# A preceding attention layer with a mixture of experts: the router on an exact fp32 input, the shared expert last, and all engines' orders rewritten

## The chip, the cores and the metric

The kernel runs on one core of a Trainium2 chip. Its time is the device time of one execution in microseconds; 136.29 us is the median of three runs of the kernel before (136.12 to 136.59).

## The reference

x has shape (2, 1024, 128), fp32. Two pre-normed blocks follow each other.

```python
x = x + attention(layernorm(x))   # 4 heads, q/k 32 wide with rotary, v 64 wide
# retention: o = (q k^T * decay_mask) v, rms-normalised per head, gated by silu(x Wg^T), times Wo^T
x = x + ffn(layernorm(x))
def ffn(x):
    shared = silu(x @ sh_up_w + sh_up_b) @ sh_down_w + sh_down_b
    scores = softmax(x @ gate_w.T)                # 8 experts
    topk_w, topk_i = top_k(scores, 2); topk_w = topk_w / topk_w.sum()
    comb = one_hot(topk_i) weighted by topk_w     # (tokens, 8)
    y = sum over e of comb[:, e] * (silu(x @ up_w[e] + up_b[e]) @ down_w[e] + down_b[e])
    return y + shared
```

## The kernel before, in words

The 1024 positions of the two sequences are cut into four groups (g = 0 to 3) of four tiles of 128 tokens; a pair (g, p), p = 0 or 1, is the same 128 positions of both sequences. Every engine has its own program: a list of calls of small functions, written out by hand in one order for each engine (POOL from L394, ACT from L550, DVE from L934, PE from L1290). Semaphores join them. In PE's list an `after(signal, g, p)` waits for a signal before the call behind it; most such waits are there so that a PSUM bank is free again. The dictionary `PLACE` (L48) says in which PSUM bank the result of each attention step goes, `OWN` (L63) where it goes otherwise.

Attention, for each pair: `x1_t` transposes the normed input on PE, ACT's `x1_hi` copies it from PSUM rounded to fp32r (XH1), DVE's `x1_lo` writes the rest (XL1). `proj_qk`, `proj_v` and `proj_g` each make three fp32r matmuls per tile (high by high, high by low, low by high: `product`, L1100 to L1104). Rotary and `rotate` are on DVE, `qk_t` transposes (PE) and ACT's `qk_sb` copies. Then `scores` (PE, bank set bA), `masked` (DVE, reads bA), `attend` (PE, writes bA), `squares` (ACT) and `gate_out` (DVE), which both read bA; the next `scores` waits for `gate_out` (`after(ogr, ...)`). POOL does the reciprocal roots and `normalize_out`, then come `out_t` (PE), `transposed_out` (ACT), `proj_out` (PE), `add_attention` (DVE).

Experts, for each group: `stats2`, the norm, `x2_t` on PE, `x2_hi` on ACT (L498, fp32r copy XH2) and `x2_lo` on DVE (L821, XL2). `router` (L1208) multiplies each of the four tiles, as the stationary operand, with the router weights: two fp32r matmuls per tile, XH2 by the 16 columns GWS (high and low) and XL2 by the 8 high ones. `route_a` (L826) adds the two parts of the logits on DVE and takes the maximum off, `exps` on ACT makes the exponentials, `rank` and `route_b` on DVE choose two experts and make the weights CMB and CX, `comb_t` (PE) transposes them, `comb_rows` and `comb_sb` (ACT) copy them out. SP broadcasts the rows through DRAM into CB (`widen`, L295). `up_proj(g, k)`, k = 0 to 8, makes three fp32r matmuls with 512 columns, ACT's `hidden` applies SiLU, DVE's `gating` multiplies by CB. k = 0 is the shared expert, which takes no weight (`expert`, L242). `down_proj` adds all nine in bank bY by fp32 matmuls. ACT's `sums`, PE's `y_t` and DVE's `result` give the output of groups 0 to 2.

Group 3 has another ending. `down_last` (L1236) multiplies tile by tile, tokens on the partitions. The shared expert (k = 0) and the biases (`bias`, L1259) go to bY; `base` (L898) adds the residual X into YS; `mix(3, k)`, k = 1 to 8 (L904), adds each routed expert's product from bank k mod 4 of bA, scaled by its column of CMB, four DVE instructions (L922) per expert, the last ones into OUT. `store_last(0)` and `store_last(1)` (L313) send the halves from the SP queue.

In ACT's list `exps` needs the exponential table and the `hidden` behind it the SiLU table: each change is an ACT_TABLE_LOAD.

Of the kernel before, what the change touches and what calls it, by code (L numbers as in the profile page):

```python
# [40 lines left out]
TABLES = 6  # L41
# [56 lines left out]
def retention_moe_kernel(nc, x, wqkvg, wot, gnw, upw, upb, dnw, dnb, gatew, const, rotary_tables, scratch, out):  # L98
    ctx = ExitStack()
    with ctx:  # L100
# [6 lines left out]
        def sig(name, per=1):  # L107
# [18 lines left out]
        GWS = sb("GWS", [P, 2, E], F32R)  # L126
# [36 lines left out]
        XL2 = sb("XL2", [P, 2, GC], F32R)  # L163

# [19 lines left out]
        YS = sb("YS", [P, GC])  # L184
        OUT = sb("OUT", [P, 2, TILES, P])
# [14 lines left out]
        w_ex_hi, gw_lo, uw_lo, wog, db_hi, db_lo = (  # L200
            sig(n) for n in ("w_ex_hi", "gw_lo", "uw_lo", "wog", "db_hi", "db_lo"))
# [15 lines left out]
        biased, based, mixed, last_half, tail = (sig(n) for n in ("biased", "based", "mixed", "last_half", "tail"))  # L217
# [24 lines left out]
        def expert(k):  # L242
            return E if k == 0 else k - 1
# [20 lines left out]
        def _(sp):  # L264
# [61 lines left out]
            store_last(1)  # L326
# [4 lines left out]
        def _(pool):  # L331
# [73 lines left out]
            rstd1(3, 1)  # L405
            rms(0, 1)
            normalize_out(0, 1)
            rms(1, 0)
            normalize_out(1, 0)
            rstd2(0, 0)  # L410
            rstd2(0, 1)
            rms(1, 1)
            normalize_out(1, 1)
            rstd2(1, 0)
# [5 lines left out]
            rstd2(2, 0)  # L420
            rms(3, 0)
            rstd2(2, 1)
            normalize_out(3, 0)
            rms(3, 1)
            normalize_out(3, 1)
            rstd2(3, 0)
# [3 lines left out]
        def _(act):  # L430
# [67 lines left out]
            def x2_hi(g, p):  # L498
                act.wait_ge(t4.sem, t4.at(g, p))
                act.copy(XH2[:, g % 2, two(p)], place("x2_t", g, p)[:, 0:2 * P]).then_inc(xh2.sem, 1)  # L500

            def hidden(g, k):
                e = expert(k)
# [34 lines left out]
            def split_experts():  # L538
                act.wait_ge(ld_gw.sem, 16)
                act.copy(GWS[:, 0, :], GW[:, :])  # L540
                act.wait_ge(ld_up.sem, 16)
                act.copy(UWH[:, :], UW[:, :]).then_inc(w_ex_hi.sem, 1)

            def split_biases():
# [3 lines left out]
                act.wait_ge(ld_ub.sem, 16)  # L548

# [14 lines left out]
            gates(1, 0)  # L564
            split_biases()
            x1_hi(1, 1)
            squares(0, 0)
            values(1, 0)
            values(1, 1)
            qk_sb(1, 0)  # L570
            x1_norm(2, 0)
            x1_norm(2, 1)
            gates(1, 1)
            x1_hi(2, 0)
            transposed_out(0, 0)
# [74 lines left out]
            hidden(2, 5)  # L650
            x2_norm(3, 0)
            hidden(2, 6)
            x2_norm(3, 1)
            x2_hi(3, 0)
            x2_hi(3, 1)
            hidden(2, 7)
            hidden(2, 8)
# [5 lines left out]
            hidden(3, 3)  # L663
            hidden(3, 4)
            comb_sb(3)
# [3 lines left out]
            hidden(3, 8)  # L669

        @block.vector
        def _(dve):
# [153 lines left out]
            def route_a(g):  # L826
                parts = bM[:, 0:TILES * 2 * E].rearrange("r (m s e) -> r m s e", s=2, e=E)
                dve.wait_ge(logits.sem, logits.at(g))
                dve.tensor_reduce(LG[:, :, :], parts.rearrange("r m s e -> r m e s"), AX.X, ALU.add).then_inc(route_a_step.sem, 1)
# [68 lines left out]
            def base(g):  # L898

                dve.wait_ge(biased.sem, 1)  # L900
                dve.wait_ge(yt.sem, yt.at(g - 1))
                dve.tensor_tensor(YS[:, :], bY[:, :], X[:, g * GC:(g + 1) * GC], ALU.add).then_inc(based.sem, 1)

            def mix(g, k):  # L904
                if k == 1:
                    dve.wait_ge(based.sem, 1)
                    dve.wait_ge(route_b_step.sem, route_b_step.at(g, 4))
                if k < E:
                    dve.wait_ge(down.sem, down.at(g, k))
# [181 lines left out]
        def _(pe):  # L1091
# [116 lines left out]
            def router(g):  # L1208
                pe.wait_ge(xl2.sem, xl2.at(g, 1))
                if g == 0:  # L1210
                    pe.wait_ge(gw_lo.sem, 1)
# [378 lines left out]
```

## Time and profile before

| | us |
|---|---|
| median of three runs | 136.29 |
| the profiled execution | 136.48 |
| its span in the profile | 134.7 |
| PE busy | 128.8 |
| DVE busy | 102.9 |
| ACT busy | 81.2 |
| POOL busy | 43.6 |

The span runs from the first to the last thing that the profile shows; 1.8 us of the execution lie outside. PE is the matmul engine, PEld its weight loads, DVE the vector engine, ACT the scalar engine, SP the engine that issues most DMAs. A busy PE record contains the matmul's pipeline, so records overlap: what one matmul costs in a stream is the distance from its start to the next start. One fp32 matmul stands as two records with a weight load each (`proj_out` makes 4 matmuls for each of 8 pairs, and L1197 has 40 + 16 + 8 = 64 records), one fp32r matmul and one transpose as one. The chain of waits gives, from the last instruction backwards, which piece of work set the time.

### The profile page before, as it was taken

The numbers are of one execution on the slowest core, as the hardware profiler recorded it, in microseconds if no ns is written. First come the engines' busy times: TensorE is split into PE (matmuls) and PEld (weight loads), VectorE is DVE, ScalarE is ACT, GpSimd is POOL, SyncE is SP. The second block draws the span as 40 slices with busy tenths as digits, with TensorE's granted clock in tenths as the row PEclk, the third lists the DMA queues.
The fourth block names the chain that finished last, engine by engine and source line by source line (L and its number), as shares of the span: only waits on it lengthen the run. The fifth ranks groups of instructions, "written<-read, shape, count | busy, mean of one in ns | idle before, by whom it ended". The sixth has DMA issues, their size and how long they took to land.

```text
span 134.7 us, 3595 instructions
## 1 busy us (share of the span) xinstructions
PE 128.8 (96%) x1359; PEld 101.7 (76%) x1359; DVE 102.9 (76%) x318; ACT 81.2 (60%) x146; POOL 43.6 (32%) x64
## 2 busy tenths in 40 slices
PE   5999899999999999999999999999999999999990
PEld 5897798999899988978665588566676557489980
DVE  3889999999999999995997728966249437425983
ACT  3359959677506369977848355977454834980230
POOL 6534599390707738264321107000004200000000
PEclk9999999999999999999999999999999999999998
DMA  4999900000000000009900593000961100002002
GB/s 108 290 372 336 335 24 0 5 0 7 5 0 5 0 5 0 2 12 287 339 1 5 146 403 136 21 0 27 324 277 40 42 2 0 0 15 65 5 0 78
DMA packets 8661, 12.53 MB, mean 93 GB/s; under 512 B 1298, under 2 KB 5676, under 8 KB 8644
## 3 DMA queue, kind: packets, MB, share of 16 engines
q1 hardware_dynamic: 8212, 11.84, 26.4%
q10 hardware_dynamic: 432, 0.46, 1.2%
q8 instruction: 11, 0.18, 0.5%
q14 instruction: 6, 0.05, 0.1%
HBM read 11.20 MB, written 1.10 MB: 91 GB/s over the span
## 4 chain that ended last, share of the span: by engine, by line
PE 81%; DVE 7%; ACT 4%; DMA 4%; issue 2%; ACTq 1%; DVEq 0%
PE bY L1281 16%; PE bU L1102 9%; PE bU L1104 8%; PE bU L1103 8%; PE bA L1178 6%; PE bA L1254 5%; DMA W<-wqkvg 4%; PE bU L1197 3%; PE bA L1146 2%; PE bA L1172 2%; PE bU L1138 2%; PE bY L1102 1%; PE bM L1215 1%; PE bM L1197 1%; PE bM L1217 1%
## 5 line engine op out<-in xcount | busy, mean ns | idle before, releaser
L509 ACT ACTIVATE HB<-bU,UB 128x512 f32<-128x512 f32 x36 | 24.6, 687 | 22.2 <-PE bU L1104 21.5
L884 DVE TENSOR_TENSOR HG<-CB,HB 128x512 f32<-128x512 f32 x24 | 16.9, 719 | 11.1 <-ACT HB L509 7.2
L1281 PE MATMUL bY<-HG,DW 128*128 128x512 f32 x48 | 24.6, 594 | 0.0
L1102 PE MATMUL bU<-XH,UWH 128*128 128x512 f32 x36 | 22.6, 628 | 0.2 <-ACT HB L509 0.2
L355 POOL TENSOR_TENSOR RR<-SS,NHALF 128x8 f32<-128x8 f32 x8 | 13.1, 1642 | 17.3 <-DVE SS L779 17.2
L1103 PE MATMUL bU<-XL,UWH 128*128 128x512 f32 x36 | 14.2, 395 | 0.0
L1104 PE MATMUL bU<-XH,UWL 128*128 128x512 f32 x36 | 14.2, 394 | 0.0
L369 POOL TENSOR_SCALAR VE<-MV 128x2 f32<-128x2 f32 x8 | 2.2, 281 | 29.2 <-DVE MV L804 29.2
L1102 PEld LDWEIGHTS bU<-XH,UWH 128*128 128x128 f32 x36 | 6.8, 189 | 5.4 <-issue 4.9
L760 DVE TENSOR_TENSOR SC<-bA,MASK 128x512 f32<-128x512 f32 x16 | 10.2, 680 | 0.1
L484 ACT ACTIVATE SQ<-bA 128x512 f32<-128x512 f32 x8 | 4.8, 598 | 8.9 <-PE bA L1178 8.9
L1103 PEld LDWEIGHTS bU<-XL,UWH 128*128 128x128 f32 x36 | 6.8, 190 | 4.1 <-issue 4.1
L1281 PEld LDWEIGHTS bY<-HG,DW 128*128 128x128 f32 x48 | 8.6, 189 | 1.6
L362 POOL TENSOR_TENSOR OG<-OGR,RR 128x512 f32<-128x512 f32 x8 | 8.4, 1045 | 3.7 <-issue 3.2
L1178 PE MATMUL bA<-V,SC 128*64 128x64 f32 x256 | 9.2, 225 | 0.0
L1102 PE MATMUL bU<-WH,XH 128*128 128x256 f32 x28 | 9.0, 321 | 0.0
L1178 PEld LDWEIGHTS bA<-V,SC 128*64 128x64 f32 x256 | 8.1, 138 | 0.7 <-issue 0.2
L1254 PE MATMUL bA<-DW,HB 128*128 128x128 f32 x64 | 8.2, 277 | 0.0
L1254 PEld LDWEIGHTS bA<-DW,HB 128*128 128x128 f32 x64 | 7.8, 191 | 0.3
L1104 PEld LDWEIGHTS bU<-XH,UWL 128*128 128x128 f32 x36 | 6.8, 188 | 1.6
L1103 PE MATMUL bU<-WL,XH 128*128 128x256 f32 x28 | 7.9, 284 | 0.0
L1104 PE MATMUL bU<-WH,XL 128*128 128x256 f32 x28 | 7.9, 282 | 0.0
(171 smaller groups left out, 312.3 us busy)
## 6 DMA issues: line engine op xcount, KB each, us to landing
CB<-scratch SPq DMA_DIRECT2D x12, 512.0 KB, 5.3
ROT<-rotary_tables SPq DMA_DIRECT2D x8, 256.0 KB, 4.7
out<-OUT SPq DMA_DIRECT2D x8, 128.0 KB, 1.8
X<-x SPq DMA_DIRECT2D x7, 128.0 KB, 4.7
UW<-upw SPq DMA_DIRECT2D x1, 576.0 KB, 4.8
DW<-dnw SPq DMA_DIRECT2D x1, 576.0 KB, 4.1
W<-wqkvg ACTq DMA_DIRECT2D x1, 256.0 KB, 4.9
W<-wqkvg ACTq DMA_DIRECT2D x1, 128.0 KB, 3.4
```

The lines of the kernel that those rows point to most:

```text
L355: pool.tensor_tensor(RR[:, n], SS[:, n], NHALF[:, 0:2 * H], ALU.pow).then_inc(rr.sem, 1)
L362: pool.tensor_tensor(OG[:, p].rearrange("r (n v) -> r n v", v=DV), OGR[:, p].rearrange("r (n v) -> r n v", v=DV), RR[:, pair(g, p)].unsque ...
L509: act.activation(HB[:, k, :], bU[(g * (E + 1) + k) % 2][:, :], ACT.Silu, bias=UB[:, e:e + 1]).then_inc(hid.sem, 1)
L760: last = dve.tensor_tensor(SC[:, p, h:h + 2], bA[:, h:h + 2, 0:2 * P].rearrange("r h (b n) -> r h b n", b=2), MASK[:, h:h + 2, :].unsqueez ...
L884: dve.tensor_tensor(HG[:, k % RING, :], CB[:, k - 1, :], HB[:, k, :], ALU.mult).then_inc(gated.sem, 1)
L1102: pe.matmul(out_, ah, bh, start=start, stop=False)
L1103: pe.matmul(out_, ah, bl, start=False, stop=False)
L1104: return pe.matmul(out_, al, bh, start=False, stop=stop)
L1178: last = pe.matmul(bA[q, h, b * DV:(b + 1) * DV], SC[:, p, h, b, q], V[:, slot(g, p), b, h * DV:(h + 1) * DV], start=(n == 0 and b == 0), ...
L1197: last = pe.matmul(place("proj_out", g, p)[:, b * P:(b + 1) * P], OGT[:, p, b, a, :], WOG[:, a, :], start=(a == 0), stop=(a == 1))
L1254: last = pe.matmul(dst, HB[:, k, t], DW[:, e * P:(e + 1) * P], start=first, stop=final)
L1281: pe.matmul(bY[:, :], DW[:, e * P:(e + 1) * P], HB[:, 0, :] if k == 0 else HG[:, k % RING, :], start=(k == 0), stop=(k == E)).then_inc(dow ...
```

## The change

The router reads a new buffer XF2, the transposed normed input in fp32, which ACT copies from PSUM besides XH2. It multiplies each tile by GW in one fp32 matmul with 8 columns. GWS is gone, with its ACT copy and its POOL subtraction; `route_a` copies the logits instead of adding two parts. `x2_hi` waits for the logits of the group before, since XF2 has one buffer. TABLES, the number of rotary buffers, goes from 6 to 5.

In group 3 the shared expert is k = 8 instead of k = 0. `mix(3, k)` runs for k = 0 to 7 and starts from X. The biases and the shared expert go together to bY (tiles 0 and 1) and bM (tiles 2 and 3), and `final` adds them to YM in two DVE instructions of 256 columns. `base` is gone. The second half of group 3 is stored from ACT's queue.

PLACE and the lists of all four engines are written anew. PE's list has the same 174 calls in another order; its end is shown below, and of the others the places that the text speaks of.

```diff
-TABLES = 6
+TABLES = 5
         def expert(g, k):
+            if g == LAST:
+                return k
             return E if k == 0 else k - 1
             def low_experts():
-                pool.tensor_tensor(GWS[:, 1, :], GW[:, :], GWS[:, 0, :].bitcast(F32), ALU.subtract).then_inc(gw_lo.sem, 1)
             def x2_hi(g, p):
                 act.wait_ge(t4.sem, t4.at(g, p))
+                if g:
+                    act.wait_ge(logits.sem, logits.at(g - 1))
+                act.copy(XF2[:, two(p)], place("x2_t", g, p)[:, 0:2 * P])
                 act.copy(XH2[:, g % 2, two(p)], place("x2_t", g, p)[:, 0:2 * P]).then_inc(xh2.sem, 1)
             def split_experts():
-                act.wait_ge(ld_gw.sem, 16)
-                act.copy(GWS[:, 0, :], GW[:, :])
             def route_a(g):
-                dve.tensor_reduce(LG[:, :, :], parts.rearrange("r m s e -> r m e s"), AX.X, ALU.add).then_inc(route_a_step.sem, 1)
+                dve.tensor_copy(LG[:, :, :].rearrange("r m e -> r (m e)"), bM[:, 0:TILES * E]).then_inc(route_a_step.sem, 1)
-            def base(g):
-                dve.wait_ge(biased.sem, 1)
-                dve.wait_ge(yt.sem, yt.at(g - 1))
-                dve.tensor_tensor(YS[:, :], bY[:, :], X[:, g * GC:(g + 1) * GC], ALU.add).then_inc(based.sem, 1)
+                    before_ = YM[:, t] if k else X[:, g * GC + m * P:g * GC + (m + 1) * P]
+                    dve.scalar_tensor_tensor(out=YM[:, t], in0=bA[:, k % 4, t], scalar=CMB[:, m, k:k + 1], in1=before_,
+                                             op0=ALU.mult, op1=ALU.add).then_inc(mixed.sem, 1)
+            def final(g):
+                dve.wait_ge(stored[g - 2].sem, 32)
+                for h, src in enumerate((bY, bM)):
+                    if h == 0:
+                        dve.wait_ge(last_half.sem, 1)
+                    else:
+                        dve.wait_ge(down.sem, down.at(g, E))
+                    dve.wait_ge(mixed.sem, TILES * (E - 1) + 2 * h + 2)
+                    dve.tensor_tensor(OUT[:, g % 2, 2 * h:2 * h + 2].rearrange("r m n -> r (m n)"), src[:, two(h)], YM[:, two(h)],
+                                      ALU.add).then_inc(tail.sem, 1)
             def router(g):
-                pe.wait_ge(xl2.sem, xl2.at(g, 1))
+                pe.wait_ge(xh2.sem, xh2.at(g, 1))
-                    pe.matmul(bM[:, o:o + 2 * E], XH2[:, g % 2, t], GWS[:, :, :].rearrange("r s e -> r (s e)"),
-                              start=True, stop=False)
-                    last = pe.matmul(bM[:, o:o + E], XL2[:, g % 2, t], GWS[:, 0, :], start=False, stop=True)
+                    last = pe.matmul(bM[:, m * E:(m + 1) * E], XF2[:, t], GW[:, :], start=True, stop=True)
```

PE's list from `comb_t(0)` to `scores(3, 0)`, before: `comb_t(0)`, `up_proj(0, 3)`, `scores(3, 0)`. After: `comb_t(0)`, `up_proj(0, 3)`, `x2_t(1, 0)`, `qk_t(3, 0)`, `x2_t(1, 1)` (behind `ct_sb`), `proj_g(3, 1)`, `up_proj(0, 4)`, `out_t(2, 1)`, `scores(3, 0)` (behind `sg(3, 1)`, that is ACT's `gates(3, 1)`).
ACT's list there, after: `hidden(0, 2)`, `comb_rows(0)`, `comb_sb(0)`, `x2_hi(1, 0)`, `qk_sb(3, 0)`, `x2_hi(1, 1)`, `gates(3, 1)`, `hidden(0, 3)`.

PE's list from the last router on:

```text
before: router(3) up(3,0) down(2,6) up(3,1) down(2,7) up(3,2) down(2,8) up(3,3) up(3,4) y_t(2) comb_t(3)
        up(3,5) dl(0) dl(1) bias dl(2) dl(3) up(3,6) dl(4) dl(5) up(3,7) dl(6) up(3,8) dl(7) dl(8)
after:  up(3,0) router(3) down(2,6) up(3,1) down(2,7) up(3,2) down(2,8) dl(0) up(3,3) y_t(2) dl(1) comb_t(3)
        dl(2) up(3,4) dl(3) up(3,5) dl(4) up(3,6) dl(5) up(3,7) dl(6) up(3,8) dl(7) bias dl(8)
```

(up is up_proj, down is down_proj, dl(k) is down_last(3, k).) ACT's list there is the same in both but for `comb_sb(3)`: `hidden(3, 0)`, `exps(3)`, `hidden(3, 1)`, `hidden(3, 2)`, `sums(2)`, `hidden(3, 3)`.

Between the first `attend` and the second `scores` PE had `proj_v(1, 0)`, `state_add(0, 1)`, `proj_v(1, 1)`, `qk_t(1, 0)`, `state_add(1, 0)`, and has `state_add(0, 1)`, `proj_g(1, 0)`, `proj_g(1, 1)`. In DVE's list `add_attention(0, 0)`, `stats2(0, 0)` and `normalize2(0, 0)` move from behind `rotary(3, 0)` to between `rotary(2, 0)` and `mean_squares(1, 0)`.

## Rows read from the trace of the kernel before

**Rows 1.** The page: busy time, and the chain of waits by engine.

```profile
PE 128.8 (96%) x1359; PEld 101.7 (76%) x1359; DVE 102.9 (76%) x318; ACT 81.2 (60%) x146; POOL 43.6 (32%) x64
...
PE 81%; DVE 7%; ACT 4%; DMA 4%; issue 2%; ACTq 1%; DVEq 0%
```

**Rows 2.** Busy time by stretch: length, engines' busy us, clock, DMA share, GB/s.

```profile
14.50:30.00 15.50, 15.46 (x245) 13.99 (x246) 15.30 (x47) 11.76 (x27) 12.17 (x14) 1.00 0.17 60
30.00:50.00 20.00, 19.95 (x391) 17.92 (x389) 19.50 (x55) 9.87 (x20) 8.60 (x12) 1.00 0.01 4
50.00:62.00 12.00, 11.90 (x210) 10.15 (x206) 10.55 (x36) 9.99 (x17) 7.09 (x8) 1.00 0.13 32
```

**Rows 3.** Timeline of PE at router(3): start us, us, engine, line.

```profile
110.75 0.57 PE L1215 MATMUL bM<-GWS,XH 128*128 128x16 f32 x1
111.17 0.25 PE L1217 MATMUL bM<-GWS,XL 128*128 128x8 f32 x1
...
111.96 0.47 PE L1102 MATMUL bU<-XH,UWH 128*128 128x512 f32 x1
```

**Rows 4.** Chain of waits, fp32 matmuls: start us, us, what, records.

```profile
50.22 1.09 PE bY L1197 x8
...
84.05 0.86 PE bY L1281 x2
...
102.39 0.36 PE bM L1156 x16
```

**Rows 5.** Groups by form: busy, mean ns, idle before.

```profile
L500 ACT CAST XH<-bM 128x256 fp32r<-128x256 f32 x6 | 2.2, 368 | 1.9 <-PE bM L1205 1.9
L540 ACT CAST GWS<-GW 128x8 fp32r<-128x8 f32 x1 | 0.2, 227 | 0.0
L375 POOL TENSOR_TENSOR GWS<-GW,GWS 128x8 fp32r<-128x8 f32 x1 | 0.2, 208 | 2.0 <-ACT UWH L542 2.0
L829 DVE TENSOR_REDUCE LG<-bM 128x32 f32<-128x64 f32 x4 | 0.9, 218 | 0.2 <-PE bM L1217 0.2
L793 DVE TENSOR_TENSOR X<-bY,X 128x256 f32<-128x256 f32 x1 | 0.4, 416 | 0.0
```

**Rows 6.** Timeline around the tables of exps(3).

```profile
112.62 0.19 DVE L833 TENSOR_TENSOR SHI<-LG,MX 128x32 f32<-128x32 f32 x1
...
113.63 1.28 ACT L513 ACT_TABLE_LOAD   x1
...
116.06 1.02 PE L1281 MATMUL bY<-HG,DW 128*128 128x512 f32 x2
...
116.47 1.27 ACT L509 ACTIVATE HB<-bU,UB 128x512 f32<-128x512 f32 x2
...
117.30 0.47 PE L1102 MATMUL bU<-XH,UWH 128*128 128x512 f32 x1 [0.22 <-ACT HB L509]
```

**Rows 7.** Chain of waits, its last part.

```profile
118.95 0.44 PE bY L1287 x4
...
122.30 0.40 PE bY L1263 x4
...
124.53 0.23 PE bU L1102
...
125.22 1.78 PE bA L1254 x16
...
129.30 0.91 PE bA L1254 x8
```

**Rows 8.** Timeline of the end.

```profile
130.23 1.13 DVE L922 SCALAR_TENSOR_TENSOR YS<-bA,CMB,YS 128x128 f32<-128x128 f32 x4 [0.45 <-PE bA L1254]
131.27 1.12 DVE L922 SCALAR_TENSOR_TENSOR OUT<-bA,CMB,YS 128x128 f32<-128x128 f32 x4
131.90 0.89 SPq L316 DMA_DIRECT2D out<-OUT  x2
```

**Rows 9.** Timeline of ACT at comb_rows(0).

```profile
57.12 0.58 ACT L519 COPY CR<-bM 32x512 f32<-32x512 f32 x1
```

More of the change, by code:

```diff
@@ L1349, in _ @@
+            after(st, 0, 1)
+            state_add(1, 0)
+            after(xl1, 1, 0)
+            x1_t(2, 0)
+            attend(0, 1)
+            after(st, 1, 0)
+            out_t(0, 0)
+            after(rparts, 1, 1)
+            x1_t(2, 1)
+            after(v_sb, 1, 1)
+            qk_t(1, 0)
+            after(xl1, 2, 0)
+            state_add(1, 1)
+            after(ogt, 0, 0)
+            proj_qk(2, 0)
+            after(qkt, 1, 0)
+            proj_out(0, 0)
             after(ogr, 0, 1)
@@ L1372, in _ @@
+            proj_out(0, 1)
             after(ogr, 1, 0)
             scores(1, 1)
+            after(x1, 0, 1)
+            proj_g(2, 1)
+            after(xl2, 0, 0)
+            state_add(2, 0)
+            after(qkt, 2, 0)
+            proj_qk(2, 1)
+            after(sg, 2, 1)
+            out_t(1, 0)
+            after(qkt, 1, 1)
+            x1_t(3, 0)
+            attend(1, 1)
+            after(rparts, 2, 1)
+            proj_out(1, 0)
+            after(ogt, 1, 0)
+            qk_t(2, 1)
@@ L1374, in _ @@
+            after(xl1, 3, 0)
+            x2_t(0, 1)
             after(st, 2, 0)
             state_add(2, 1)
[L1376 to L1389 removed]
@@ L1408, in _ @@
+            proj_g(3, 0)
+            after(x1, 1, 0)
+            x1_t(3, 1)
+            after(xl2, 0, 1)
+            proj_v(3, 0)
+            after(sg, 3, 0)
+            proj_qk(3, 0)
+            attend(2, 0)
+            after(rparts, 3, 0)
+            out_t(1, 1)
+            after(st, 2, 1)
+            router(0)
+            after(v_sb, 3, 0)
             up_proj(0, 0)
@@ L1422, in _ @@
+            proj_out(2, 0)
             after(hid, 0, 2)
-            proj_g(3, 1)
-            after(xl2, 1, 0)
+            proj_qk(3, 1)
+            after(st, 3, 0)
             comb_t(0)
-            after(ogt, 2, 0)
+            after(x1, 2, 0)
             up_proj(0, 3)
+            after(ogt, 1, 1)
+            x2_t(1, 0)
             after(ogr, 2, 1)
-            scores(3, 0)
+            qk_t(3, 0)
             after(ct_sb, 0)
             x2_t(1, 1)
-            after(sg, 3, 1)
-            proj_out(2, 0)
@@ L1434, in _ @@
-            after(hid, 0, 3)
-            qk_t(3, 1)
-            after(sg, 3, 0)
-            out_t(2, 1)
-            attend(3, 0)
-            after(x1, 2, 0)
-            up_proj(0, 4)
-            after(ogt, 2, 1)
-            state_add(3, 0)
+            after(ogr, 2, 1)
+            proj_g(3, 1)
+            after(rparts, 3, 1)
+            up_proj(0, 4)
+            after(xl2, 1, 0)
+            out_t(2, 1)
+            after(ogr, 2, 1)
+            after(sg, 3, 1)
+            scores(3, 0)
@@ L1460, in _ @@
             down_proj(0, 5)
-            up_proj(0, 8)
+            up_proj(1, 3)
             down_proj(0, 6)
-            after(ct_sb, 1)
-            x2_t(2, 0)
+            up_proj(1, 4)
+            down_proj(0, 7)
+            after(route_a_step, 2, 0)
+            out_t(3, 0)
+            up_proj(1, 5)
+            down_proj(0, 8)
+            up_proj(1, 6)
+            after(ogt, 3, 0)
+            comb_t(2)
+            up_proj(1, 7)
+            after(hid, 1, 6)
+            qk_t(3, 1)
@@ L1465, in _ @@
+            y_t(0)
+            after(ct_sb, 2)
+            proj_out(3, 0)
+            down_proj(1, 0)
             after(ogr, 3, 0)
             scores(3, 1)
-            down_proj(0, 7)
-            after(xl2, 2, 0)
-            x2_t(2, 1)
-            down_proj(0, 8)
-            attend(3, 1)
-            up_proj(1, 0)
-            after(xl2, 2, 1)
-            out_t(3, 0)
-            up_proj(1, 1)
-            y_t(0)
-            up_proj(1, 2)
-            after(ogt, 3, 0)
-            router(2)
@@ new lines, in _ @@
+            up_proj(2, 0)
+            down_proj(1, 3)
+            after(hid, 1, 8)
+            x2_t(3, 0)
+            down_proj(1, 4)
+            attend(3, 1)
+            down_proj(1, 5)
+            after(xl2, 3, 0)
+            up_proj(2, 1)
+            down_proj(1, 6)
+            up_proj(2, 2)
+            down_proj(1, 7)
+            up_proj(2, 3)
+            down_proj(1, 8)
+            after(hid, 2, 3)
+            out_t(3, 1)
+            up_proj(2, 4)
+            y_t(1)
+            after(ogt, 3, 1)
@@ L1532, in _ @@
+            after(x1, 3, 0)
+            router(3)
+            down_proj(2, 6)
+            after(st, 3, 1)
             up_proj(3, 1)
```

527 lines of the change are left out of this document (224 added, 303 removed), and 26 rows, old and new, of the table PLACE.

## The prediction

> **What bounds the kernel now.** The page comes first: PE is busy for 96% of the span and 81% of the chain that ended last is PE's [rows 1]. So the chain is PE's own list, and a change is worth what it takes off that list, off PE's waits, or off what stands behind PE's last matmul. Busy time by stretch says how much waiting there is. From 14.5 to 62 us PE is busy for 15.46 + 19.95 + 11.90 = 47.31 of 47.5 us, so 0.19 us at most is idle there; but DVE has 34.80 of the 35.5 us to 50 us, and ACT 9.99 of the 12 us from 50 to 62 [rows 2]. Two other engines stand right beside PE: it is the bound, with hardly any cover. The timeline near the end shows two places where PE's list is not what sets the time. At 116 us PE's last `down_proj` record starts 0.43 us behind the one at 116.06, ends at 116.92, and the next `up_proj` starts at 117.30: 0.38 us of waiting for `hidden(3, 1)`, which ACT could start only after two table loads [rows 6]. And behind `down_last(3, 7)`, which ends at 129.30 + 0.91 = 130.21 us [rows 7], DVE works on until 131.27 + 1.12 = 132.39 us, 2.18 us later [rows 8].
>
> **The profiled execution** took 136.48 us, 0.19 us above the median of 136.29; 1.8 us of it lie outside the span and stay. The sum below is made against 136.48, and 0.19 is taken off at its end. I take 0.3% of the time, 0.4 us, as what a measurement can tell from no change.
>
> **The change part by part.**
>
> *Router on PE.* Before: eight fp32r matmuls. From the second one at 111.17 to the next `up_proj` at 111.96 are seven steps in 0.79 us, 0.11 each; eight are 0.90 us [rows 3]. They have 16 and 8 columns, so their columns don't set this; the weight load of 128 columns in front of each does. After: four fp32 matmuls. One fp32 matmul is two records with a load each, and eight records with 128-column loads and 128 moving columns take 1.09 us at most, 0.11 to 0.14 a record [rows 4]. With 8 moving columns they can't take longer; so eight records, 0.9 us, the same as before. Bound above: 1.1 us, +0.2 for each of four routers, +0.8. Bound below: fp32 records with 32-column loads take 0.36 / 16 = 0.02 each [rows 4], 0.2 us for a router, 0.7 saved, -2.8 for four. The kinds with full-width loads are nearer, so I take 0.
>
> The Trainium skill, "TensorE: Matmul & The Clock Gate", section "LDWEIGHTS (loading the stationary operand)", says that a load costs its columns by 1.2 GHz, 107 ns for 128, whatever the rows; the 0.11 us steps agree, and that rule too leaves 0 where the number of loads stays at eight. The same skill, "FP8 and Floating Point Precision", section "TensorE Precision Notes", has true fp32 as four passes through the array. If each pass took a load of its own, a router would have 16 and lose where it was meant to win; that is a rival below, and the two records per matmul speak against it.
>
> *Copies into XF2.* Eight more ACT copies from PSUM of 256 columns. The nearest row is the same copy to fp32r, 0.37 us [rows 5]: 2.96 us on ACT, which has 53 us idle in all [rows 1]. Seven of eight places have cover. The place without is the one around `comb_t(0)`. From its end to `scores(3, 0)` PE has `up_proj` 0.69, `x2_t` 0.22, `qk_t` 0.44, `x2_t` 0.22, `proj_g` 0.69, `up_proj` 0.69 and `out_t` 0.44: 3.39 us. (`up_proj` is 125.22 - 124.53; `proj_g` streams the same number of columns; four transposes take 0.44 [rows 7], two the half.) ACT must do in the same time `comb_rows`, `comb_sb`, `qk_sb`, `gates(3, 1)`, each about 0.58 [rows 9], and twice `x2_hi` at 2 x 0.37 [rows 5]: 3.80 us. `scores(3, 0)` is queued behind `gates(3, 1)`, and all of PE's list behind `scores`. The wait is 0.41, up to 0.5 with the semaphores, or 0 if PE itself comes late there: I take +0.25 between 0 and 0.5. The copy also holds up `x2_lo` by 0.37 each time; for group 3, PE has two `down_proj` (0.86 each [rows 4]) between `x2_t(3, 1)` and the `up_proj(3, 0)` that needs it, against 2 x 0.37 + 0.42 of copies: covered.
>
> *Removed work.* The ACT copy of GWS (0.23) and POOL's subtraction (0.21) stood around 14 us [rows 5], beside PE work; worth 0. Uncovered they could give back 0.2. The logits' reduction (0.22, four times [rows 5]) becomes a copy of about the same length; 0.
>
> *TABLES, queues.* Rotary loads 5 to 7 wait for one rotary step more. They stand before the first `widen` in SP's list, and each waits for a rotary step that lies four pairs or more ahead of the one that needs the table. 0. The x2_hi wait for the logits of the group before: that router stands before the `x2_t` of the group in PE's list, so it has been done. 0.
>
> *Shared expert last.* Behind `down_last(3, 7)` DVE now has `mix(3, 7)`, 1.13 us [rows 8], and two additions of 256 columns, 2 x 0.42 by the nearest row, one of PSUM and SBUF [rows 5]: 1.97 instead of 2.18 us. PE meanwhile does the bias, 0.40 [rows 7], and `down_last(3, 8)`, 0.89: 1.29, earlier than 1.13 + 0.42. And since the bias now stands behind `down_last(3, 7)`, that one ends 0.40 us sooner. Gain 0.21 + 0.40 = 0.61. `base`, which waited for the bias, is gone; `mix(3, k)` has 0.69 + 0.89 = 1.58 us of PE work per expert against its 1.13, so DVE arrives in time. Bounds: 0.2 if DVE is still catching up after `result(2)`, 0.9 if the half stored from ACT's queue lands sooner by the spacing of the two issues (0.89 for two [rows 8]). I take -0.6.
>
> *The stall at 117 us.* `up_proj(3, 0)` now stands before the last router and `down_last(3, 0)` before `up_proj(3, 3)`. From the router's end PE has 5 pieces (three of 0.86, two of 0.69), the bias matmul of group 2 (0.24) and `down_last(3, 0)` (0.89): 5.1 us. ACT needs for `hidden(3, 1)`: 0.85 until SHI is there (112.81 against 111.96 [rows 3, 6]), two table loads and the exponentials 2.84 (116.47 - 113.63), one `hidden` about 0.7: 4.4 us. The wait of 0.38 us goes; next late would be `sums(2)`, 1.3 us behind, against `y_t(2)`, 0.7 us behind: even. I take -0.38, between 0 and -0.38.
>
> *The new order from 14.5 to 62 us.* The same calls in another order; 0.19 us of idle PE is all that can be won. I take 0 and keep -0.2 to +0.6 for the range.
>
> **Sum:** 136.48 + 0.25 - 0.61 - 0.38 = 135.74 us; less 0.19 gives 135.55, say **135.6 us**.
>
> **The rivals.**
>
> *B, one load per tile.* If one fp32 matmul with 8 columns takes one load, a router has four instead of eight: 4 x 0.11 saved, 1.8 us for four routers, 133.8 us. For it: no 8-column fp32 matmul is in the trace. Against: all fp32 kinds have two records each. 0.07.
>
> *E, a load per pass.* Sixteen loads instead of eight, 0.88 us more per router, 3.5 us: 139.1 us. Against it, the same rows. 0.03.
>
> *C, slower: ACT becomes the bound between 50 and 60 us.* Place: `proj_out(2, 0)`, `proj_qk(3, 1)` and `scores(3, 0)`, which wait for `transposed_out(2, 0)`, `hidden(0, 2)` and `gates(3, 1)`. Price: the four copies of groups 0 and 1 come onto PE's path, 4 x 0.37 = 1.48, on top of the 0.25: 135.55 + 1.48 = 137.0 us. It decides from where ACT reaches `comb_rows(0)` over 0.5 us behind `comb_t(0)`. For it: ACT is 83% busy there before the copies are added [rows 2]. Against: `exps(0)` comes earlier in the new order, so ACT's row starts ahead. 0.17.
>
> *D, nothing net.* DVE is as full as PE until 50 us [rows 2]. Between the first `attend` and the second `scores` PE now has 0.36 + 2 x 0.69 = 1.74 us of other work instead of 2.54, while `squares` (about 0.6) and `gate_out` (256 columns take 0.42 [rows 5], so 512 up to 0.8) stand between, and `add_attention` and `stats2` of group 0 are pulled in before other pairs' masks. Three such places at 0.25 give 0.75 back: 136.3 us. 0.20. That the change does not do what it says is no separate case: B and E are that.
>
> **How the numbers follow.** Forecast 0.53, B 0.07, E 0.03, C 0.17, D 0.20. Faster by over 0.3% are the forecast and B, 0.60; the same is D, 0.20; slower are C and E, 0.20. The forecast with its bounds spans 134.8 to 136.2; the range goes down to 134.4, since the router's price is bounded only from far, and up to 137.1 so that it holds C. It leaves out B, E and some 0.08 at the edges.
>
> **What the profile after would show.** Router records 0.11 us apart, eight per router (other: B or E). A last `down_last(3, 8)` behind a bias, and DVE's last instruction some 0.7 us behind PE's. No gap before `up_proj(3, 3)`. A gap of a few tenths before `scores(3, 0)`, with ACT without idle time before it. PE busy in all but 0.2 to 0.4 us of 14.5 to 62 us. Wrong would be: PE idle for over 0.8 us in that stretch, released by ACT (C) or DVE (D).

## The result, and the profile after

The kernel after takes 137.34 us (median of 22 runs, 136.87 to 139.12), the kernel before on the same chips 136.56 us (22 runs): the ratio is 1.0072 [1.0055, 1.0089], 0.7% slower. Now and then an execution falls into a slower state, which the ratios and their 95% intervals, here and below, leave out, so that they differ by up to 0.2% from the quotient of two medians. The forecast of 135.6 us was wrong, in sign too; on the scale of the 136.29 us shown ahead, after is 137.3, just past the upper end of the range.

| | before, us | after, us |
|---|---|---|
| the profiled execution | 136.48 | 137.86 |
| its span | 134.7 | 136.1 |
| PE busy | 128.8 | 129.4 |
| DVE busy | 102.9 | 103.9 |
| ACT busy | 81.2 | 82.9 |
| POOL busy | 43.6 | 42.8 |

The page of after, busy time and the chain by engine, against [rows 1]:

```profile
PE 129.4 (95%) x1359; PEld 101.8 (75%) x1359; DVE 103.9 (76%) x319; ACT 82.9 (61%) x153; POOL 42.8 (31%) x63
...
PE 75%; DMA 9%; DVE 8%; issue 2%; ACT 2%; ACTq 1%; DVEq 0%
```

PE's share of the chain falls from 81 to 75%, and DMA's rises from 4 to 9%. Busy time by stretch of after, with the columns of [rows 2]:

```profile
14.50:30.00 15.50, 15.31 (x265) 13.46 (x258) 15.28 (x44) 9.84 (x22) 11.24 (x11) 1.00 0.16 59
30.00:50.00 20.00, 20.00 (x373) 17.76 (x371) 18.90 (x57) 12.24 (x26) 9.10 (x12) 1.00 0.02 4
50.00:62.00 12.00, 12.00 (x160) 10.25 (x158) 11.13 (x38) 9.89 (x19) 7.37 (x8) 1.00 0.04 7
62.00:75.00 13.00, 12.30 (x129) 8.70 (x123) 10.64 (x34) 10.10 (x19) 1.99 (x3) 1.00 0.47 160
```

Until 62 us PE is as busy as before. The gap is behind it, from 62 to 75 us, where PE has 12.30 of 13.00 us; before it had all 13.00. The chain of waits of after shows what set that stretch:

```profile
57.56 0.45 PE bM L1224 x4
...
58.64 2.22 DMA scratch<-CR
60.88 4.13 DMA CB<-scratch
65.03 0.69 DVE HG L894
...
68.88 0.88 ACT XN L496 x2
```

`comb_t(0)` in this chain starts a round trip through DRAM of 2.22 + 4.13 = 6.35 us. DVE's `gating(0, 1)` (HG) stands in its list where the rows have not come yet, and behind it are queued `route_a(1)`, `stats2(2, 1)`, `rank(1)`, `gating(0, 2)` and `x2_bias(2, 1)`. So ACT gets the bias of pair (2, 1) late. The wait for the rows themselves is only 0.36 us of that; the rest is the work that DVE has ahead of the bias. DVE's, ACT's and PE's rows there, from the timeline:

```profile
65.03 0.69 DVE L894 TENSOR_TENSOR HG<-CB,HB 128x512 f32<-128x512 f32 x1 [0.36 <-DMA CB<-scratch]
...
67.84 0.23 ACT L519 ACTIVATE EX<-SHI 128x32 f32<-128x32 f32 x1
68.88 0.88 ACT L496 ACTIVATE XN<-X,NM,RS 128x128 f32<-128x128 f32 x2 [0.81 <-DVE NM L829]
69.78 1.28 ACT L515 ACT_TABLE_LOAD   x1
71.07 1.26 ACT L515 ACTIVATE HB<-bU,UB 128x512 f32<-128x512 f32 x2
...
70.67 1.02 PE L1279 MATMUL bY<-HG,DW 128*128 128x512 f32 x2
...
72.39 0.44 PE L1209 MATMUL bU<-IDN,XN 128*128 128x128 f32 x2 [0.70 <-ACT HB L515]
```

`x2_norm(2, 1)` (L496) stands between the exponentials and the SiLU table, waits 0.81 us, and `hidden(0, 7)` and `hidden(0, 8)` wait with it. PE's `x2_t(2, 1)` needs the bank that `hidden(0, 8)` reads: it starts 1.72 us behind `down_proj(0, 2)`, which takes 0.86, so 0.86 us are lost.

The router and the ending are as they were meant to be. The router is eight records at 114.41, and the next `down_proj` starts 0.81 us later:

```profile
114.41 0.95 PE L1218 MATMUL bM<-GW,XF 128*128 128x8 f32 x8
115.22 1.11 PE L1279 MATMUL bY<-HG,DW 128*128 128x512 f32 x2
...
116.86 1.28 ACT L515 ACT_TABLE_LOAD   x1
...
119.51 1.05 PE L1252 MATMUL bA<-DW,HB 128*128 128x128 f32 x8
...
120.32 0.47 PE L1106 MATMUL bU<-XH,UWH 128*128 128x512 f32 x1
```

`down_last(3, 0)` runs while ACT changes tables, and `up_proj(3, 3)` follows without a gap; the 0.38 us of [rows 6] are gone. The end of after, against [rows 8]:

```profile
131.90 1.12 DVE L918 SCALAR_TENSOR_TENSOR YM<-bA,CMB,YM 128x128 f32<-128x128 f32 x4 [0.46 <-PE bA L1252]
132.09 0.66 PE L1252 MATMUL bY<-DW,HB 128*128 128x128 f32 x4
132.59 0.61 PE L1252 MATMUL bM<-DW,HB 128*128 128x128 f32 x4
132.94 0.41 DVE L930 TENSOR_TENSOR OUT<-bY,YM 128x256 f32<-128x256 f32 x1
133.27 0.41 DVE L930 TENSOR_TENSOR OUT<-bM,YM 128x256 f32<-128x256 f32 x1
```

DVE ends at 133.68, 0.48 us behind PE's last record (133.20); before it ended 1.15 us behind PE (132.39 against 129.14 + 2.10 = 131.24).

### The profile page after: what moved, and what is told of

Its sections match the earlier page's. It is cut to its first block, busy times and chain, and to the rows that moved or that the text cites. A ratio compares the mean times of both kernels' runs of the same rounds, so it can differ in the third digit from the quotient of the medians.

```text
span 136.1 us, 3608 instructions
## 1 busy us (share of the span) xinstructions
PE 129.4 (95%) x1359; PEld 101.8 (75%) x1359; DVE 103.9 (76%) x319; ACT 82.9 (61%) x153; POOL 42.8 (31%) x63
## 4 chain that ended last, share of the span: by engine, by line
PE 75%; DMA 9%; DVE 8%; issue 2%; ACT 2%; ACTq 1%; DVEq 0%
PE bY L1279 16%; PE bU L1106 7%; PE bU L1108 7%; PE bU L1107 7%; PE bA L1182 6%; PE bA L1252 5%; DMA W<-wqkvg 4%; DMA CB<-scratch 3%; PE bU L1201 3%; PE bA L1150 3%; PE bY L1106 2%; PE bM L1218 2%; PE bA L1176 2%; PE bU L1142 2%; DMA scratch<-CR 2%
## 5 line engine op out<-in xcount | busy, mean ns | idle before, releaser
L1106 PE MATMUL bU<-XH,UWH 128*128 128x512 f32 x36 | 22.1, 615 | 0.0
L358 POOL TENSOR_TENSOR RR<-SS,NHALF 128x8 f32<-128x8 f32 x8 | 13.6, 1696 | 23.8 <-DVE SS L790 23.6
L918 DVE SCALAR_TENSOR_TENSOR YM<-bA,CMB,YM 128x128 f32<-128x128 f32 x28 | 7.9, 344 | 2.7 <-PE bA L1252 2.7
L1106 PE MATMUL bU<-WH,XH 128*128 128x256 f32 x26 | 8.0, 306 | 0.2 <-DVE WL L906 0.2
L1107 PE MATMUL bU<-WL,XH 128*128 128x256 f32 x26 | 7.3, 281 | 0.0
```

Of the source, the lines that this page charges most:

```text
L358: pool.tensor_tensor(RR[:, n], SS[:, n], NHALF[:, 0:2 * H], ALU.pow).then_inc(rr.sem, 1)
L918: dve.scalar_tensor_tensor(out=YM[:, t], in0=bA[:, k % 4, t], scalar=CMB[:, m, k:k + 1], in1=before_, op0=ALU.mult, op1=ALU.add).then_inc( ...
L1106: pe.matmul(out_, ah, bh, start=start, stop=False)
L1107: pe.matmul(out_, ah, bl, start=False, stop=False)
```

## The experiments

The kernels were run in four groups, each beside its own runs of before on the same chip: e1 to e4, e5 to e8, e9 to e12, e13 to e16. PE's stretch is the time from the start of `qk_t(0, 1)` to the start of `down_last(3, 0)`. PE makes the same calls in it in every kernel with the new ending (e14 alone has one call less), so it can be compared across orders.

| kernel | ratio to before | PE's stretch, us |
|---|---|---|
| after; again (e15) | 1.0072 [1.0055, 1.0089]; 1.0079 [1.0049, 1.011] | 104.56; 104.62 |
| e1, router alone | 0.9997 [0.9972, 1.0021] | (old ending) |
| e2, ending alone | 0.989 [0.9864, 0.9916] | 102.39 |
| e3, both; again (e16) | 0.9903 [0.9872, 0.9934]; 0.9923 [0.9895, 0.9952] | 102.39; 102.43 |
| e4, ACT's order | 1.0004 [0.998, 1.0027] | 103.77 |
| e5, e4 and DVE's start | 1.0022 [1.0004, 1.0039] | 104.19 |
| e6, e4 and calls joined | 1.0023 [1.0004, 1.0042] | 103.82 |
| e7, e3 with calls split | 0.9952 [0.9934, 0.997] | 103.01 |
| e9, DVE's order | 1.0038 [1.002, 1.0056] | 104.28 |
| e10, ACT's and DVE's | 0.9994 [0.9975, 1.0014] | 103.69 |
| e11, old router | 1.0064 [1.0038, 1.009] | 104.82 |
| e12, all repairs | 0.9993 [0.9971, 1.0015] | 103.54 |
| e13, e3, one join | 0.9915 [0.9886, 0.9944] | 102.25 |
| e14, e13, no last state | 0.9872 [0.9843, 0.9902] | 101.98 |

### The two edits without the new lists

**e1** makes the router edit (XF2, one fp32 matmul per tile, the copied logits, TABLES 5) in the lists and with the PLACE of before.

> The router edit alone: fp32 router, XF2 copies, copied logits, five rotary tables, in the lists of the kernel before. If the loss lies in the rewritten lists (my theory now), this is within 0.4 us of the kernel before. If the eight ACT copies cost by themselves, it is 0.5 to 1.5 us slower, with PE waiting for ACT between 50 and 62 us.

**e2** makes the ending alone: the shared expert last in group 3, `mix` from X, `final`, the second store from ACT's queue, and in the lists only what these need. PE's list is after's from `down_proj(2, 8)` on.

> The ending alone: shared expert last, final, the second store from ACT's queue, and PE's list of the changed kernel only from down_last(3, 0) on. My terms say -0.61 for the end and -0.38 for the stall at 117 us, 1.0 us faster. The rival, that the ending gives nothing because the last store sets the time, says within 0.3 us of the kernel before.

**e3** is both edits at once: all that follows from them, and nothing of the new order ahead of the ending.

```diff
             down_proj(2, 8)
+            down_last(3, 0)
             up_proj(3, 3)
-            up_proj(3, 4)
             y_t(2)
+            down_last(3, 1)
             comb_t(3)
...
-            down_last(3, 7)
-            down_last(3, 8)
+            down_last(3, 7)
+            bias(3)
+            down_last(3, 8)
```

> Router edit and ending together, all other lists as in the kernel before. If the rewritten lists are the loss: 0.8 to 1.0 us faster than the kernel before, so about 1.9 us faster than the changed kernel. If the two edits disturb each other: no faster than the kernel before.

The router alone changes nothing measurable: 136.50 us. The ending alone takes off 1.1% [0.84, 1.36]. Both together give 135.33 us, the same as the ending alone within the intervals. So neither edit costs anything that these runs can tell, and the 2.0 us between e3 and after lie in what is left of the diff: PLACE and the new order of all four engines' lists. No run takes PLACE and the lists apart; "the new lists" below means both. The end of e2, from the timeline:

```profile
130.04 0.61 PE L1256 MATMUL bM<-DW,HB 128*128 128x128 f32 x4
130.40 0.41 DVE L931 TENSOR_TENSOR OUT<-bY,YM 128x256 f32<-128x256 f32 x1
130.72 0.41 DVE L931 TENSOR_TENSOR OUT<-bM,YM 128x256 f32<-128x256 f32 x1
```

PE ends at 130.65 instead of 131.24, DVE 0.48 us behind it instead of 1.15.

**e11** asks the same from the other side: after with the fp32r router of before, all new lists kept.

```diff
-                act.copy(XF2[:, two(p)], place("x2_t", g, p)[:, 0:2 * P])
-                    last = pe.matmul(bM[:, m * E:(m + 1) * E], XF2[:, t], GW[:, :], start=True, stop=True)
+                    pe.matmul(bM[:, o:o + 2 * E], XH2[:, g % 2, t], GWS[:, :, :].rearrange("r s e -> r (s e)"),
+                              start=True, stop=False)
+                    last = pe.matmul(bM[:, o:o + E], XL2[:, g % 2, t], GWS[:, 0, :], start=False, stop=True)
```

> The kernel after with the fp32r router of before (XH2 and XL2 by GWS, no XF2, the logits' reduction): all new lists, PLACE and the new ending kept. Theory (the router edit is worth nothing in either list): the time of after within 0.3%. Rival (the copies into XF2 are what the fuller ACT list can't hide): 0.4 to 1.5 us less than after.

137.51 us, 1.0064: the time of after. The eight copies cost nothing measurable in the new lists either.

### The stall at 71 us

**e4** moves one call in ACT's list.

```diff
             exps(1)
-            x2_norm(2, 1)
             hidden(0, 7)
             hidden(0, 8)
+            x2_norm(2, 1)
```

> The changed kernel with one ACT call moved: x2_norm(2, 1) behind hidden(0, 8) instead of between exps(1) and hidden(0, 7). In the changed kernel PE waits for hidden(0, 8) before x2_t(2, 1), at 71 to 72.4 us, 0.9 us. If ACT's wait for x2_bias(2, 1) ahead of the table load is its cause, PE gets 0.6 to 0.9 us back and the ratio to the kernel before falls from 1.007 to about 1.001 to 1.003. If the wait only moves on (x2_t(2, 1) then waits for x2_norm), it stays at 1.007.

136.72 us against 136.57 for before. ACT now takes the SiLU table at once, and PE's gap is gone:

```profile
68.10 0.23 ACT L519 ACTIVATE EX<-SHI 128x32 f32<-128x32 f32 x1
68.35 1.28 ACT L515 ACT_TABLE_LOAD   x1
69.64 1.27 ACT L515 ACTIVATE HB<-bU,UB 128x512 f32<-128x512 f32 x2
70.80 0.87 ACT L496 ACTIVATE XN<-X,NM,RS 128x128 f32<-128x128 f32 x2
...
71.81 0.41 PE L1209 MATMUL bU<-IDN,XN 128*128 128x128 f32 x2
```

PE's stretch falls by 0.79 us, the ratio by 0.7%: the stall was worth about what the trace shows. Behind it `up_proj(1, 1)` now comes 0.29 us late, and `router(2)`, which was late in after, is not: these two nearly cancel.

**e9** leaves ACT as it is in after and changes DVE's list.

```diff
-            gating(0, 1)
-            route_a(1)
             stats2(2, 1)
+            route_a(1)
+            gating(0, 1)
```

> The kernel after with one place of DVE's list changed: gating(0, 1), route_a(1), stats2(2, 1) becomes stats2(2, 1), route_a(1), gating(0, 1). Theory (gating(0, 1) waits for the rows of CMB that come back through DRAM, and stats2(2, 1), queued behind it, makes x2_norm(2, 1), the SiLU table and two hidden late for x2_t(2, 1)): the reciprocal root of pair (2, 1) starts about 1.4 us earlier, PE's gap of 0.86 us ahead of x2_t(2, 1) goes, and the time falls by about 0.8 us against after, ratio to before 1.001. Rival (the two table loads of ACT are what is late, not DVE): the gap stays above 0.5 us and the ratio above 1.005.

The first half of the theory holds: POOL's root starts at 65.23 instead of 67.04. The second doesn't: PE still loses 0.54 of the 0.86 us.

```profile
67.50 0.23 ACT L519 ACTIVATE EX<-SHI 128x32 f32<-128x32 f32 x1
68.22 0.88 ACT L496 ACTIVATE XN<-X,NM,RS 128x128 f32<-128x128 f32 x2 [0.48 <-DVE NM L829]
69.11 1.28 ACT L515 ACT_TABLE_LOAD   x1
```

DVE's `gating(0, 1)` doesn't wait for the DMA here, yet `x2_norm` still stands ahead of the table load, and its bias still waits behind `rank(1)` and `gating(0, 2)` on DVE, as in after. So most of the stall is ACT's order (e4) and the work that DVE has ahead of the bias, and not the wait for the round trip. The ratio of 1.0038 lies between the two forecasts.

**e10** is e4 and e9 together.

> e4 (x2_norm(2, 1) behind hidden(0, 8) on ACT) with the same change of DVE's list. Theory (DVE's wait for the DMA also makes comb_t(1) and up_proj(1, 1) late, 0.3 us in e4 and 0.5 in e5): 0.3 to 0.5 us less than e4, and up_proj(1, 1) starts about 0.4 us behind comb_t(1) instead of 0.64. Rival (these waits come from PE's own order): the time of e4.

`up_proj(1, 1)` starts 0.36 us behind `comb_t(1)` as expected (e4: 0.65), but by `up_proj(1, 2)` all but 0.05 us is given back as a wait ahead of `router(2)`. 136.56 us: no change that can be told from e4.

### The start

**e5** is e4 with the start of DVE's list as before.

```diff
-            x1_lo(0, 0)
             low_w(0)
+            x1_lo(0, 0)
```

> The kernel after with ACT's x2_norm(2, 1) moved (run e4) and the old start of DVE's list: low_w(0) before x1_lo(0, 0). Theory (part of the lost time is a later start: the first proj_qk begins at 6.71 us and qk_t(0, 1) at 14.95 to 15.2 us instead of 14.3 to 14.55, because DVE writes WL after XL): proj_qk(0, 0) begins at 6.3 to 6.5 us, qk_t(0, 1) at about 14.5, and the time falls by 0.3 to 0.5 us against e4. Rival (the second load of W simply landed later in those executions, whatever the list): the cast of the 512 columns of WH still begins behind 7.0 us, qk_t(0, 1) stays at 15, and the time is that of e4.

The theory fails. `proj_qk(0, 0)` starts at 6.67 us and not at 6.3, and the time is that of e4. `proj_v(0, 0)` starts when the second load of W has landed, in the profiled executions anywhere from 7.82 (e1) to 8.98 us (e12); e12 has the same start of DVE's list as e5, which has 8.11, and the same kernel has 8.51 in after and 8.11 in e15. What the landing varies with was not found. The second thing e5 shows is worth more: PE ran 0.66 us ahead of e4 until 73 us, and then lost 0.45 of it: `comb_t(1)` came 0.18 later than in e4, reckoned from the start of the stretch, and `up_proj(1, 1)` another 0.28. `gating(0, 1)` came only 0.21 us earlier than in e4 (65.65), since the round trip took longer:

```profile
58.23 0.30 SPq L302 DMA_DIRECT2D scratch<-CR  x1
...
65.44 0.69 DVE L894 TENSOR_TENSOR HG<-CB,HB 128x512 f32<-128x512 f32 x1 [1.18 <-DMA CB<-scratch]
```

It is 7.21 us from the first issue to DVE's start here, 6.39 in after and 6.76 in e4; DVE stands idle for 1.18, 0.36 and 0.72 us of it. In these three the DMA's return sets the time at that place, whatever PE did ahead of it.

### The small-matmul calls

`scores`, `state_add` and `attend` use 32 or 64 rows or columns of the array. The lists of e3 put 22 such calls into 18 groups in PE's stretch, those of after into 20.

**e8** measures the price of going there and back by itself, on the identity, ahead of e3's list.

```diff
+            keep_busy(16)
+            for _ in range(12):
+                tiled(4)
+                keep_busy(4)
+            tiled(48)
+            keep_busy(48)
```

> e3 with a test in front of the list of PE, on the identity alone: 16 full matmuls to warm up, then twelve times four 32-row matmuls and four full ones, then 48 of the one and 48 of the other. Theory (a price per excursion): the alternating stretch is longer than the grouped one by 11 excursions, 2.2 to 3.0 us. Rival (free): both stretches have the same length within 0.2 us.

```profile
7.28 0.50 PE L1292 MATMUL bA<-IDN 32*128 32x128 f32 x8
7.71 1.16 PE L1099 MATMUL bA<-IDN 128*128 128x128 f32 x8
8.80 0.50 PE L1292 MATMUL bA<-IDN 32*128 32x128 f32 x8
...
25.54 2.96 PE L1292 MATMUL bA<-IDN 32*128 32x128 f32 x96
28.43 12.55 PE L1099 MATMUL bA<-IDN 128*128 128x128 f32 x110
40.81 0.38 PE L1115 MATMUL bU<-IDN,XN 128*128 128x128 f32 x2
```

The alternating stretch takes 25.54 - 7.28 = 18.26 us. The grouped one takes 2.89 for the small ones and 12.38 us for 110 full records (14 of them are the `keep_busy(7)` behind), so 10.80 for 96: 13.69. The difference is 4.57 us for 11 excursions, 0.4 each, above the 0.2 to 0.27 expected. It is one execution, with matmuls of 32 rows alone.

**e7** splits two groups in e3.

```diff
-            x1_t(3, 0)
             state_add(1, 1)
+            x1_t(3, 0)
             state_add(2, 0)
             scores(1, 1)
-            state_add(2, 1)
             x1_t(3, 1)
+            state_add(2, 1)
```

> e3 with two pairs of small-matmul calls taken apart: x1_t(3, 0) now stands between state_add(1, 1) and state_add(2, 0), x1_t(3, 1) between scores(1, 1) and state_add(2, 1). Same calls, same work. Theory (an excursion costs 0.2 to 0.27 us): 0.4 to 0.5 us more than e3. Rival (free): the time of e3.

PE's stretch grows by 0.62 us and the time by 0.42 us between the medians (135.33 and 135.75, on two chips; by the ratios against e16 and e3 it is 0.4 and 0.7). Not all of it is the price of an excursion. The bank of `x1_t(3, 1)`, which now stands directly behind `scores(1, 1)`, is still read by `x1_lo(3, 0)` on DVE:

```profile
35.17 0.73 PE L1151 MATMUL bA<-QKT 32*128 32x128 f32 x16
...
36.04 0.20 PEld L1115 LDWEIGHTS bU<-IDN,XN 128*128 128x128 f32 x2 [0.34 <-DVE XL L729]
```

So `scores(1, 1)` takes 0.87 us to the next call, where `scores(2, 0)`, in front of a transpose of the same kind that doesn't wait, takes 0.66 in the same trace. Without these 0.21 us the two excursions cost 0.41 us of PE's stretch, 0.2 each.

**e6** joins three in e4.

```diff
-            state_add(1, 0)
             x1_t(2, 0)
+            state_add(1, 0)
             attend(0, 1)
...
             scores(1, 1)
-            proj_g(2, 1)
             state_add(2, 0)
+            proj_g(2, 1)
...
             attend(2, 1)
+            state_add(3, 0)
             out_t(2, 0)
             up_proj(0, 2)
-            state_add(3, 0)
```

> e4 with three state_add calls moved to stand beside another call of small matmuls: state_add(1, 0) directly before attend(0, 1), state_add(2, 0) directly behind scores(1, 1), state_add(3, 0) directly behind attend(2, 1). Theory (each excursion of PE into tiles of fewer than 128 rows or columns and back costs about 0.2 to 0.27 us): three excursions fewer, 0.6 to 0.8 us less than e4, 136.0 us. Rival (no price for an excursion; the calls cost the same anywhere): no change against e4.

No gain. The first join saves 0.14 us. At the second, PE now comes too early for the bank, which `x2_lo(0, 0)` still reads:

```profile
34.75 0.73 PE L1150 MATMUL bA<-QKT 32*128 32x128 f32 x16
35.67 0.43 PE L1160 MATMUL bM<-V,QKR 128*32 128x64 f32 x16 [0.19 <-DVE XL L834]
36.03 0.39 PE L1106 MATMUL bY<-WH,XH 128*128 128x256 f32 x1
```

It gives back 0.27, and the third 0.05. An excursion saved where the next wait ends late is worth nothing.

**e12** takes e4, e9's order, e5's start and the first join.

> After with all the repairs at once: x2_norm(2, 1) behind hidden(0, 8), stats2(2, 1) and route_a(1) ahead of gating(0, 1), low_w(0) ahead of x1_lo(0, 0), state_add(1, 0) directly ahead of attend(0, 1). Theory (after's loss is a sum of places in its lists): 0.86 + 0.3 + 0.2 + 0.15 = 1.5 us less than after, ratio 0.996, still 0.5 us behind e3. Rival (the places hide each other): no better than e4 and e10.

136.57 us, 0.9993: nearer to the rival. PE's stretch is the shortest of all with the new lists, 103.54 us, but only 1.02 below after, and its W landed last. Repairs one by one bring after back to before, not to e3.

**e13** and **e14** join and remove in e3. e14 leaves out the last update of the attention state, which no later `attend` reads.

```diff
             attend(3, 0)
+            state_add(3, 0)
             up_proj(0, 4)
-            state_add(3, 0)
...
-            state_add(3, 1)
```

> e3 with state_add(3, 0) moved from behind up_proj(0, 4) to directly behind attend(3, 0): one excursion of PE into small matmuls fewer, at a place where no wait ends late. Theory (an excursion costs 0.2 to 0.3 us): 0.2 to 0.3 us less than e3. Rival (the price was that of the waits around it): the time of e3.

> e13 without the last state update, state_add(3, 1) on PE and state(3, 1) on DVE, which no later attend reads. Theory: one excursion fewer with its 16 small matmuls, 0.25 + 0.3 = 0.55 us less on PE than e13. Rival (PE waits for another engine there): under 0.2 us less.

Here no wait is near, and e13's stretch is 0.18 us shorter than e16's in the same group, the cleanest measure of one excursion. From `up_proj(0, 4)` and `state_add(3, 0)` to `down_proj(0, 0)` it is 64.28 - 62.11 = 2.17 us in e16 and 64.14 - 62.16 = 1.98 in e13. The times, 135.25 and 135.41 us, can't be told apart. e14 is 134.68 us, 1.3% [1.0, 1.6] below before and the fastest found. The whole update cost PE 0.31 us at its place, against 0.55 expected. The medians of e14 and e13 are 0.57 us apart. In the profiled executions PE ends 0.46 us sooner in e14: its stretch is 0.27 shorter, and it began 0.20 sooner (`qk_t(0, 1)` at 14.39 against 14.59), which is no gain of the edit, since that start varies. The rest is not explained.

**e15** and **e16** are after and e3 again, on one chip.

> The kernel after once more, on the same chip. Theory: ratio 1.007, 2.2 to 2.4 us above e3, and PE's gap ahead of x2_t(2, 1) again 0.8 to 0.9 us. If the arrival of the second load of W is what varies, proj_v(0, 0) starts somewhere between 8.0 and 9.0 us, whatever the list.

> e3 once more, on the chip on which after is run again, so that the two stand against the same runs of before. Theory (the rewritten lists cost 2.2 us: PE takes 104.6 us from qk_t(0, 1) to down_last(3, 0) in after and 102.4 in e3): ratio 0.990, and the stretch takes 102.4 us again. Rival (part of the distance between e3 and after was the chips and single executions): ratio above 0.995.

137.50 against 135.41 us, 2.1 us apart. PE's stretch repeats within 0.06 us. The stall is there again: `x2_t(2, 1)` is 0.34 us earlier than in after, from a start 0.41 us earlier. W landed at the usual time in both (8.11 and 8.10 us for `proj_v(0, 0)`), so the start is no part of the distance.

## Why the prediction was wrong

**The step that failed** is "The new order from 14.5 to 62 us. The same calls in another order; 0.19 us of idle PE is all that can be won. I take 0 and keep -0.2 to +0.6 for the range." The new lists cost 2.1 us (e15 against e16). Two things were wrong in it.

First, the window. The lists are new up to 110 us, and the step priced nothing between 62 and the last router. The largest piece lies there. PE's stretch is 104.56 - 102.39 = 2.17 us longer in after than in e3. Shown by undoing it is the stall of 0.86 us at 71 us (e4). The two additional excursions are worth 0.4 us, by the price in e7 and e13; they were not undone one by one in after. Two places in the timeline of after add 0.5 us, read there and not tried. `router(2)` waits for `comb_sb(1)`: from `down_proj(0, 4)` to `up_proj(1, 2)` it is 1.94 us, and 1.67 in e4, where the router doesn't wait. And from `out_t(3, 0)` at 82.04 to `up_proj(1, 5)` it is 0.60 us, where `out_t(3, 0)` takes 0.35 to the next `up_proj` in e3. A third wait, 0.22 us of `up_proj(2, 6)` for `add_attention(3, 1)`, costs nothing: from `down_proj(2, 0)` to `down_proj(2, 1)`, with that call between them in both kernels, it is 1.56 us in after and 1.55 in e3, which doesn't wait there. The stall, `router(2)` and this third one stand in the waits of PE's weight loads in after (us in total, times, longest; a load runs ahead, so it shows more than PE loses):

```profile
PEld bU L1209 <- ACT HB L515: 1.5, 1, 1.5
...
PEld bM L1218 <- ACT CT L531: 0.8, 1, 0.8
...
PEld bU L1106 <- DVE X L804: 0.5, 1, 0.5
```

The sum is 0.86 + 0.4 + 0.27 + 0.25 = 1.8 of 2.17 us. Where the other 0.4 us lie is open.

Second, "the same calls" was taken for the same cost wherever PE shows no idle time. It isn't. A call costs by its neighbours. From its start to the next call's, `up_proj(0, 4)` takes 0.90 us in e16, where a `state_add` follows, and 0.81 in e13, where the router follows; `router(1)` takes 0.91 behind the `state_add` of e16 and 0.81 behind the `up_proj` of e13:

```profile
63.37 1.06 PE L1219 MATMUL bM<-GW,XF 128*128 128x8 f32 x8
64.28 0.68 PE L1280 MATMUL bY<-HB,DW 128*128 128x512 f32 x1
...
63.33 0.95 PE L1219 MATMUL bM<-GW,XF 128*128 128x8 f32 x8
64.14 0.68 PE L1280 MATMUL bY<-HB,DW 128*128 128x512 f32 x1
```

(The first two rows are e16's, the others e13's.) Two different kinds of small matmuls side by side aren't free either: in e3 `state_add(1, 1)` takes 0.25 us in front of another `state_add`, and `state_add(2, 0)` 0.33 in front of `scores(1, 1)`, which takes 0.78 in front of a `state_add` and 0.66 in after in front of a projection. The busy rows can't show this. PE stood at 20.00 of 20.00 us between 30 and 50 us in after, which was read as full work. The Trainium skill, "TensorEngine Tiling (Array Packing)", section "Key Properties", says that a change of the tiling mode drains TensorE; it gives no price. e8's rows agree that a change costs time, and give a price: 0.2 us for each change, 0.4 for there and back on fp32 matmuls. In the kernel e13 and e7 have half of that.

**The other steps.**

- Router on PE, 0: right. Eight records 0.11 us apart, 0.81 us for a router; e1 gives 0.9997. The rivals B (four loads) and E (sixteen) are out: it is two per fp32 matmul, as the rows of before had it.
- Copies into XF2, +0.25 at `scores(3, 0)`: wrong by its whole size, 0 measured. `gates(3, 1)` started at 60.65 and `out_t(2, 1)` at 61.17, and `scores(3, 0)` followed 0.52 us later, the time of four transposes and the change to small matmuls: no wait. e11 has the time of after.
- Shared expert last, -0.61 and the stall, -0.38: right in mechanism, and a little more. e2 gives -1.1% or 1.5 us, its span -1.2 against -0.99. In the terms of the prediction, `down_last(3, 7)` ends 0.90 us sooner in e2 (at 128.26 + 1.05 = 129.31, against 130.21), where 0.40 for the bias and 0.38 for the stall had been forecast; and DVE ends 1.82 us behind it, not 2.18, where 1.97 had been forecast: the first addition starts 1.09 us behind it and the second 0.32 us later, not 1.13 and 0.42. The 0.38 us were themselves a rough reading: the row in [rows 6] has 0.22 us idle ahead of `up_proj(3, 3)`.
- TABLES, removed work, the queues, 0: right as a sum (e1, e11).
- Rival C, ACT as the bound from 50 to 62 us: not there. PE has 12.00 of 12.00 us (above). What did happen is C's mechanism 10 us later and without the copies: ACT waits in list order for a late value and pays two table loads around it. Rival D, DVE until 50 us, did not come either. The slow side had 0.20 of the chance, for the wrong reason.

The prediction's own test, "PE idle for over 0.8 us in that stretch", would have passed the kernel after, since it looked at 14.5 to 62 us too.

## What to carry to other kernels

When all lists are rewritten, the new order is a change of its own with its own term. Walk the whole of it for calls that wait for a DMA round trip (6 to 7 us here, for which DVE stood idle 0.4 to 1.2 us) with other work queued behind them, and for anything between an exponential and the table load behind it. Look as well at what else stands ahead of a late value: here the wait for the DMA was the smaller part, and moving ACT's one call got nearly all of the stall back. An engine at 100% busy has not shown that it does the same work in the same time: compare when it reaches the same call. And measure an edit in the old lists first: here e2 and e3 keep a gain of 1%, and the new lists cost 1.6 to 1.7%.

## What the hardware showed that was not expected

- Going from full matmuls to 32-row ones and back costs PE 0.4 us in e8's rows and about 0.2 in the kernel (0.18 in e13, 0.2 in e7), with no idle time on PE's rows.
- The time until the second load of W (256 KB) had landed varied by over 1 us between executions, `proj_v(0, 0)` from 7.82 to 8.98 us, with the same start of all lists too (8.11 in e5, 8.98 in e12). The round trip of the rows of CMB through DRAM took 6.4 to 7.2 us where DVE waited for it.
- A wait on a row of PE need not cost anything: `up_proj(2, 6)` is released 0.22 us late in after, and the call behind it starts within 0.01 us of where it does without the wait.
- A later start of 0.66 us can shrink by the end where a DMA sets the pace in between (e5 against e4: 0.66 us ahead at 60 us, 0.24 us at the last call).
